# A Perceiver block on one core: self-attention products reordered, five chunks of context values moved

## What is computed

```
x += bitnet_cross_attention(LN(x), ctx)      # ternary weights, int8 activations
x += grouped_rope_attention(LN(x))           # 16 heads of 8, 4 key/value groups, causal   "self-attention 0"
x += mixture_ffn(LN(x))                      # 8 experts merged per token, FF = 512
x += long_attention(LN(x), ctx)              # 16 heads, 32 queries against 512 context tokens
x += causal_attention(LN(x))                 # 16 heads of 8, biases                         "self-attention 1"
x += fourier_linear(LN(x))                   # one 128 x 128 matrix
```

## Time and profile before

| | |
|---|---|
| median of 3 runs | 340.75 us (339.51 to 340.79) |
| the profiled execution, its own time | 340.16 us |
| its span, first to last instruction | 338.3 us |
| mean granted TensorE clock | 0.94 of full |
| PE, DVE, ACT, POOL busy | 80%, 69%, 51%, 15% |
| self-attention 0, from its input on partitions to the sums of its last products | 124.4 to 139.7 us |
| feed-forward layer | 150 to 215 us |
| long attention, from its first query product to its last output | 219 to 299 us |
| self-attention 1 | 306.4 to 323.9 us |

### The profile page before, as it was taken

How to read it: one execution, slowest core, us unless ns; L and a number is a source line. 1 busy time by engine, 2 the same in 40 slices (tenths; PEclk the granted TensorE clock), 3 DMA queues, 4 the chain that set the end, 5 groups by cost and what they waited for, 6 DMA issues and landing times.

```text
span 338.3 us, 7625 instructions
## 1 busy us (share of the span) xinstructions
PE 269.9 (80%) x3085; PEld 163.6 (48%) x3086; DVE 233.5 (69%) x585; ACT 172.0 (51%) x316; POOL 50.7 (15%) x175
## 2 busy tenths in 40 slices
PE   0148686878787999599999999479999999949854
PEld 0113323435343778474445555237567676735742
DVE  4799999986979967349753444577778787275734
ACT  2578896875547554431012000075988888802520
POOL 3115030710000020020002000201322322120002
PEclk9999999899999999779999999987999999976965
DMA  6992000000003999691000000000000000000001
GB/s 169 225 345 100 1 2 0 1 3 2 2 2 77 212 216 241 164 408 43 4 0 0 2 0 0 0 5 0 2 4 4 2 4 4 6 2 0 2 2 31
DMA packets 6315, 19.34 MB, mean 57 GB/s; under 512 B 1157, under 2 KB 2693, under 8 KB 5253
## 3 DMA queue, kind: packets, MB, share of 16 engines
q1 hardware_dynamic: 6277, 18.82, 20.7%
HBM read 12.07 MB, written 0.26 MB: 36 GB/s over the span
## 4 chain that ended last, share of the span: by engine, by line
PE 54%; DVE 27%; ACT 8%; DMA 3%; issue 3%; POOL 3%; SPq 1%; DVEq 0%; ACTq 0%; POOLq 0%
PE PS L1129 50%; DVE sm L763 6%; DMA cx<-ctx_in 3%; DVE sm L700 2%; DVE yq L772 2%; DVE big L821 2%; DVE w L923 2%; DVE sm L922 1%; ACT sa L418 1%; POOL yq L349 1%; DVE yq L830 1%; PE PS L1336 1%; PE PS L1257 1%; ACT yq L418 1%; PE PS L1142 1%
## 5 line engine op out<-in xcount | busy, mean ns | idle before, releaser
L1077 DVE TENSOR_REDUCE sm<-PS 128x1 f32<-128x512 f32 x64 | 42.6, 687 | 14.3 <-PE PS L1129 14.1
L325 POOL TENSOR_TENSOR rstd<-veps,mhalf 128x1 f32<-128x1 f32 x24 | 12.6, 549 | 142.0 <-DVE veps L635 142.0
L1129 PE MATMUL PS<-sa,w 128*32 128x36 f32 (+1 forms) x320 | 30.8, 280 | 2.4 <-ACT w L553 2.4
L600 ACT ACTIVATE yq<-PS,sm 128x512 f32<-128x512 f32 x44 | 29.0, 685 | 5.6 <-PE PS L1129 5.2
L1129 PE MATMUL PS<-yq 128*128 128x384 f32 x96 | 31.1, 486 | 0.0
L530 ACT COPY xT<-PS 128x512 f32<-128x512 f32 x5 | 2.9, 588 | 49.5 <-PE PS L1336 49.5
L418 ACT ACTIVATE big<-PS,cols,sm 128x512 f32<-128x512 f32 (+1 forms) x32 | 26.9, 890 | 1.4 <-PE PS L1129 1.3
L1129 PE MATMUL PS<-big,yq 96*128 96x512 f16 x64 | 24.7, 391 | 2.6 <-ACT yq L418 2.6
L1129 PE MATMUL PS<-yq,big 99*128 99x128 f16 x256 | 24.7, 218 | 1.5 <-ACT yq L604 0.7
L1129 PEld LDWEIGHTS PS<-yq 128*128 128x128 f32 x96 | 18.2, 190 | 12.9 <-issue 0.5
L1129 PEld LDWEIGHTS PS<-yq,big 99*128 99x128 f16 x256 | 18.4, 97 | 11.2 <-issue 3.8
(11 more groups left out here) (253 smaller groups left out, 557.5 us busy)
## 6 DMA issues: line engine op xcount, KB each, us to landing
big<-yq SPq DMA_DIRECT2D x24, 256.0 KB, 5.1
cx<-ctx_in SPq DMA_DIRECT2D x8, 384.0 KB, 13.2
w<-w_in SPq DMA_DIRECT2D x9, 256.0 KB, 4.8
yq<-w_in SPq DMA_DIRECT2D x1, 2304.0 KB, 10.7
wa<-wa_in SPq DMA_DIRECT2D x1, 1156.0 KB, 20.0
sa<-wx_in SPq DMA_DIRECT2D x1, 768.0 KB, 16.1
rows<-rows_in SPq DMA_DIRECT2D x1, 580.0 KB, 17.7
tern<-rows_in SPq DMA_DIRECT2D x1, 512.0 KB, 8.4
```

Of the source, the lines that this page charges most:

```text
L325: pool.tensor_tensor(rstd[:, t:t + 1], veps[:, t:t + 1], mhalf[:, t:t + 1], ALU.pow)\
L600: nc.scalar.activation(pt(i), PS[:, ST_BANK[i % 2], :], ACT.Exp, scale=s1(M_ES))\
L1077: V.tensor_reduce(s1(M_MX + i % 8), PS[:, S_BANK[i % 3], :], AX, ALU.max, negate=True)\
L1129: return nc.tensor.matmul(o, lhsT, rhs, start=start, stop=stop, **kw)
```

## The change

In each self-attention PE lays the masks before it waits for `xT`, makes keys ahead of queries, and makes the values in four quarters (a bank each, in the order 6, 7, 4, 5): one before the scores, one behind them, and the last two between the transposes of the first groups. ACT expands its share of the keys before it reads the queries. It expands the values of banks 6 and 7, two operations after the second exponential and two after the third. Those of banks 4 and 5 are expanded by DVE, behind its two copies of transposed weights, under a new semaphore. The copies of transposed weights of groups 0 and 1 wait for the transposes of groups up to 1 and up to 2; those of groups 2 and 3 for their own, as before.

Of the chunks 11 to 15 of context values, three (`VALUES_AHEAD`) go ahead of the transposes of the third layer norm on PE and, on ACT, ahead of the copy that follows them; two go behind the four products of long queries on PE and behind the last head expansions on ACT. They use banks 5 and 4 in turn, no longer 6 and 5. Nothing is left of them in the loop.

Constants:

```
-                  tuple((c, 5 + c % 2) for c in range(11, NCH)))
+                  tuple((c, 4 + c % 2) for c in range(11, NCH)))
...
-        VALUE_STEPS = [(b, r) for b in range(3) for r in range(1, R)][:len(VALUES[2])]
+        VALUES_AHEAD = 3
```

ACT, the self-attention and the context values:

```
-                act.wait_ge(s["qk_ps"], 2 * k + 1)
-                affine(qTs[:, :], PS[:, 4, :], bias=col(K_Q1) if k else 0.0).then_inc(s["q_ev"], 1)
                 act.wait_ge(s["k_plain"], k + 1)
                 affine(kexp[:, 2, :], mix[:, :], scale=hm[:, 2:3]).then_inc(s["k_eva"], 1)
+                act.wait_ge(s["qk_ps"], 2 * k + 2)
+                affine(qTs[:, :], PS[:, 4, :], bias=col(K_Q1) if k else 0.0).then_inc(s["q_ev"], 1)
...
+                exponential(0)
+                exponential(1)
+                values(0, 2)
+                exponential(2)
+                values(2, 4)
+                exponential(3)
+                for r, transposed in ((1, 3), (3, 4)):
+                    act.wait_ge(s["sa_tp"], R * k + transposed)
                     nc.scalar.copy(wt[:, r, :], PS[:, r, :]).then_inc(s["sa_teva"], 1)
-                    if r == 1:
-                        values(1)
...
             nc.scalar.activation(s1(M_EXP0), s1(M_Z4), ACT.Exp)
+            for step in range(VALUES_AHEAD):
+                context_values(2, step)
             rows_to_features(3)
...
             last_heads(3)
-
+            for step in range(VALUES_AHEAD, len(VALUES[2])):
+                context_values(2, step)
```

DVE, the self-attention:

```
-                dve.wait_ge(s["qk_ps"], 2 * k + 2)
+                dve.wait_ge(s["qk_ps"], 2 * k + 1)
...
-                for r in (0, 2):
-                    dve.wait_ge(s["sa_tp"], R * k + r + 1)
+                for r, transposed in ((0, 2), (2, 3)):
+                    dve.wait_ge(s["sa_tp"], R * k + transposed)
                     V.tensor_copy(wt[:, r, :], PS[:, r, :]).then_inc(s["sa_tevd"], 1)
+                dve.wait_ge(s["v_ps"], 2 * k + 2)
+                src = PS[:, 4:6, :].rearrange("p a (b r c) -> p (a b) r c", b=4, r=R)
+                for h in range(4):
+                    V.tensor_scalar(vexp[:, 0:8, :, 8 * h:8 * h + 8], src[:, :, :, 8 * h:8 * h + 8], rm[:, h:h + 1], None,
+                                    ALU.mult).then_inc(s["v_evd"], 1)
```

PE, the self-attention (the two lines on the masks stand now ahead of the first wait) and the context values:

```
-                pe.wait_ge(s["xt_ev"], (1, 4)[k])
-                mm(PS[:, 4, :], A(q), xT[:, :]).then_inc(s["qk_ps"], 1)
-                mm(PS[:, 5, :], A(kk), xT[:, :]).then_inc(s["qk_ps"], 1)
...
                 for r in range(R):
                     mm(PS[:, r, :], identb[:, :], maskb[:, k, :].unsqueeze(1).broadcast_to([128, 4, 128]), stop=False,
                        skip_group_check=True)
+                pe.wait_ge(s["xt_ev"], (1, 4)[k])
+                mm(PS[:, 5, :], A(kk), xT[:, :]).then_inc(s["qk_ps"], 1)
+                mm(PS[:, 4, :], A(q), xT[:, :]).then_inc(s["qk_ps"], 1)
+
+                def values(n):
+
+                    bank = (6, 7, 4, 5)[n]
+                    for j in range(4):
+                        b = 4 * (bank - 4) + j
+                        last = mm(PS[:, bank, tile(j)], xrep[:, tile(b)], A(v))
+                    if n % 2:
+                        last.then_inc(s["v_ps"], 1)
...
                 values(1)
...
+                transposed(0)
+                values(2)
+                transposed(1)
+                values(3)
+                transposed(2)
+                transposed(3)
...
+            for step in range(VALUES_AHEAD):
+                context_values(2, step)
             rows_to_features(3, xn)
             pe.wait_ge(s["xt_ev"], 3)
             for r in range(R):
                 mm(PS[:, r, :], wa[:, A_WQR + 128 * r:A_WQR + 128 * r + 128], xT[:, :]).then_inc(s["lq_ps"], 1)
+            for step in range(VALUES_AHEAD, len(VALUES[2])):
+                context_values(2, step)
...
-                    if (b, r) in VALUE_STEPS:
-                        context_values(2, VALUE_STEPS.index((b, r)))
```

More of the change, by code:

```diff
@@ L550, in self_attention, with values @@
                         .then_inc(s["sa_exp"], 1)
-                for r in (1, 3):
-                    act.wait_ge(s["sa_tp"], R * k + r + 1)
+                def values(h0, h1):
+                    act.wait_ge(s["v_ps"], 2 * k + 1)
+                    src = PS[:, 6:8, :].rearrange("p a (b r c) -> p (a b) r c", b=4, r=R)
+                    for h in range(h0, h1):
+                        affine(vexp[:, 8:16, :, 8 * h:8 * h + 8], src[:, :, :, 8 * h:8 * h + 8],
+                               scale=rm[:, h:h + 1]).then_inc(s["v_ev"], 1)
+                exponential(0)
[6 more added lines that the diff above has]
+                    act.wait_ge(s["sa_tp"], R * k + transposed)
                     nc.scalar.copy(wt[:, r, :], PS[:, r, :]).then_inc(s["sa_teva"], 1)
-                    if r == 1:
-                        values(1)
                 act.wait_ge(s["ot_ps"], k + 1)
@@ L1340, in self_attention @@
                 q, kk, v, o = ("q1", "k1", "v1", "m1") if k else ("q0", "k0", "v0", "o0")
-                pe.wait_ge(s["xt_ev"], (1, 4)[k])
-                mm(PS[:, 4, :], A(q), xT[:, :]).then_inc(s["qk_ps"], 1)
-                mm(PS[:, 5, :], A(kk), xT[:, :]).then_inc(s["qk_ps"], 1)
-                def values(half):
-                    for b in range(8 * (1 - half), 8 * (2 - half)):
-                        last = mm(PS[:, 4 + b // 4, tile(b % 4)],
-                                  xrep[:, tile(b)], A(v))
-                    last.then_inc(s["v_ps"], 1)
-                pe.wait_ge(s["xrep_ok"], k + 1)
-                values(0)
                 if k == 0:
@@ L1358, in self_attention, with transposed @@
                        skip_group_check=True)
+                pe.wait_ge(s["xt_ev"], (1, 4)[k])
[8 more added lines that the diff above has]
+                        last.then_inc(s["v_ps"], 1)
+                def transposed(r):
+                    pe.wait_ge(s["sa_exp"], R * k + r + 1)
+                    for t in range(T):
+                        last = nc.tensor.transpose(PS[:, r, tile(t)], work[:, r, tile(t)], ident)
+                    last.then_inc(s["sa_tp"], 1)
+                pe.wait_ge(s["xrep_ok"], k + 1)
+                values(0)
                 pe.wait_ge(s["q_ev"], k + 1)
@@ L1369, in self_attention @@
                 values(1)
-                for r in range(R):
-                    pe.wait_ge(s["sa_exp"], R * k + r + 1)
-                    for t in range(T):
-                        last = nc.tensor.transpose(PS[:, r, tile(t)], work[:, r, tile(t)], ident)
-                    last.then_inc(s["sa_tp"], 1)
+                transposed(0)
[4 more added lines that the diff above has]
+                transposed(3)
                 pe.wait_ge(s["vones"], k + 1)
                 for half in range(2):
-                    pe.wait_ge(s["v_ev"], 8 * k + 4 * half + 4)
+                    if half:
+                        pe.wait_ge(s["v_evd"], 4 * k + 4)
+                    else:
+                        pe.wait_ge(s["v_ev"], 4 * k + 4)
                     for r in range(R):
```

14 lines of the change are left out of this document (2 added, 12 removed).

## The result

| | before | changed |
|---|---|---|
| median, 20 runs each | 340.55 us (338.67 to 341.90) | 337.3 us (333.53 to 338.99) |
| ratio | | 0.990, 95% interval 0.9879 to 0.9922 |
| span of the profiled execution | 338.3 us | 335.5 us |
| mean granted TensorE clock in it | 0.940 | 0.927 |

A forecast was written before the change was run, and what follows sets the result against it. The long cross-attention was taken as PE-bound once running, the self-attentions as bound by a chain hopping between engines. Gains 1.0 + 1.4 + 1.8 = 4.2 off 340.16 us gave 336.0, range 333.8 to 338.6.

The forecast's parts named there:

- Self-attention 0: First self-attention: scores start 0.9 sooner and the tail is 0.45 shorter, a gain of 1.35.
- Rival (c): Self-attentions: DVE's four expansions cost 0.75 each, so only the starts gain; 339.0 to 339.5, chance 0.11.
- Between: From self-attention 0 to the feed-forward layer: low clock halves work brought forward, so about 1.0 of 1.35 arrives.
- Self-attention 1: Second self-attention, at the lower clock: start gains 1.4, tail 0.45; gain taken as 1.8.
- the 5 to 6 named: Sign of being right: self-attention 1's scores start 5 to 6 us after the transposed input is copied.
- The long attention: Long cross-attention with chunks 11 to 15 out of its ramp: gain 1.4, bounds 0.3 to 2.6.
- So 2.2 of the 3.3 goes. I take back 0.8: Ramp: wait from split to first transposed scores shrinks from 3.3 to about 1.1; low clock in four transposed steps costs 0.8.
- rival (d): Start of the long cross-attention: low clock persists, 0.5 us per us; slower beyond 8.4 us more of it; chance 0.05.
- the four signs of being wrong: DVE expansions above 0.5; transposes waiting behind value quarters; half-speed transposed scores or outputs; clock low longer in total.
- Rival (b): Queries and ramp: chunks keep PE busy, so no low clock follows; gain 6.1, 334.0, chance 0.12.
- Rival (a): Ramp: scores wait for DVE's maxima and POOL's split, so it gives nothing; gain 3.0, 337.2, chance 0.20.
- The bounds of the terms: Whole kernel: the terms' lower and upper bounds together were said to give gains of 2.0 to 5.9.

The follow-up runs named there:

- sa_only: Changed kernel with the move of the context values undone, so only the self-attentions are changed; 335.9 us, ratio 0.9881.
- hold_outer: Changed kernel with 41 products of constants in PE's waits outside the ramp and none in it; 332.35 us, ratio 0.9737.
- two_in_ramp: Changed kernel with the last two moved chunks back in the ramp, behind the scores of steps 1 and 2; 336.7 us, ratio 0.9882.
- hold_clock: two_in_ramp with 8 products of constants in the ramp and 41 more in PE's other waits; 331.8 us, ratio 0.9750.
- ramp_fill: Changed kernel with 20 products of constants in PE's idle stretches of the ramp; 335.9 us, ratio 0.9883.
- after_again: The changed kernel timed once more as a control, nothing altered; 336.6 us, ratio 0.9904.
- values_only: Kernel before with only the context values moved, both self-attentions as before; 338.7 us, ratio 0.9977.

## Why the prediction was right, and where it was not

*Self-attention 0: right.* 1.35 was forecast, 1.48 measured (0.95 + 0.53). Each step holds: keys at 124.87, scores at 128.10 and released by DVE's key expansions, quarters hidden, and the last products released by DVE's value expansions. Their size, taken from the row of two 128x256 operations in the earlier trace rows, was 0.37 and is 0.41; ACT's, put at 0.37 as well where the earlier trace rows have 1.57 for four, are 0.41 too. Rival (c), at 0.75 each, is out. The Trainium skill's rule in "VectorE: DVE Perf Modes", section "Mode 2×_2P", that only a source in SBUF gives the doubled rate, agrees: from PSUM 256 elements take 0.41, where 512 from SBUF take 0.43.

*Between: right in this pair of executions.* Of 1.48, 1.18 reached the feed-forward layer (10.29 became 10.59); 1.0 was forecast of 1.35. The reason given, that work brought forward into a stretch at the lower clock runs at half speed there, is borne out by the kernels with the clock held, where this way takes 8.71 without the change and 8.73 with it, so that nothing is lost. How close 0.30 came to the 0.35 forecast is partly luck: the way took 9.3 to 10.8 in the other profiled executions without products of constants around it, by the length of the low stretch in it.

*Self-attention 1: right, and low by some 0.4.* Forecast 1.4 + 0.45, measured 1.72 + 0.48; scores start 5.1 after the input is copied, within the 5 to 6 named. The size of the start depends on the clock: transposes to scores took 7.3 to 7.8 in the kernels with the change at the lower clock. With the clock at full it is 5.90. The kernel before was not caught there with its clock up for the whole start, so what the change is worth there at full clock is not shown; the 0.95 of self-attention 0, which has the same steps, is an estimate for it.

*The long attention: wrong.* The step that failed is in the paragraph on chunks 11 to 15: "So 2.2 of the 3.3 goes. I take back 0.8". Measured, in the profiled executions, is a loss of 0.65 where a gain of 1.4 stood (0.1 to 0.65 over all of them). It has two parts. The order is worth 1.25 (77.87 with the chunks in the ramp, 76.62 with them out of it, both at full clock from the first scores on), not 2.2. The end of that step was right: without chunks, and at full clock, 1.10 lies between split and transposed scores, and 1.1 was forecast (1.39 in the changed kernel). Its start was not: of the 3.3 read off the profile, 1.0 was the lower clock under those very chunks. And the low stretch cost 2.7 (79.29 against 76.62), not 0.8: the prediction had it over with the first four transposed steps, and it went on through the start of the full pipeline, until 242. That end was named as the lower bound of the term (0.3) and, beyond it, in rival (d). Rival (d) had the right place and the wrong price: the low stretches at this place grew from 3.4 to 13.7 us, by 10.3, past the 8.4 from which (d) said that the change would lose, but each us cost about 0.2 (1.90 over 10.3, where 1.90 is 2.67 less the 0.77 by which before and sa_only differ) and not 0.5. In most of the ramp PE waits for DVE and ACT at either clock, and the 10.4 us of low clock ahead of the first outputs cost 1.4. The last 3.2, in the full pipeline, cost 1.26, that is 0.4 each, near (d)'s price.

Two of the four signs of being wrong that the prediction named were seen: transposed scores and outputs at half speed beyond the first b, and a clock that is low for longer in total (mean 0.927 against 0.940). Rival (b), that the clock holds, was seen in none of the profiled executions with the chunks moved and no products in the ramp. Rival (a), that the ramp gives nothing, has the number nearest to the median, 337.2, but not the mechanism: at full clock the order is worth 1.25 and not (a)'s 0.2, and it was the clock that took it back.

Taken together, by stages of the profiled executions the forecast was -4.2 and the measurement -2.9. The difference of 1.3 is +2.05 in the long attention and +0.30 behind it, against -0.18 in self-attention 0 and the way behind it, -0.40 in self-attention 1 and -0.46 in the tail. The 0.30 and the 0.46 are in the same program as before, where the clock changed at other moments; no step of the prediction was about them, and that they nearly cancel is luck. The bounds of the terms, added up as they stand in the prediction, give gains of about 1.9 to 6.3, not 2.0 to 5.9.

The Trainium skill's rule in "TensorE: Matmul & The Clock Gate", section "Why this matters for your kernels", that long idle gaps cost the clock, would have given the three chunks ahead of the layer norm a gain of 1 us. The trace disagrees on that place: with the gap filled up to 215.1 and a transpose at 215.42, the clock fell at 218.05 (0.52 in 218:220). The price was right where the clock did hold: in hold_outer, which has the same program there, the four products of queries took 3.70, not 5.40, and the first transposed scores came 16.65 behind the transposes, not 17.86. That the same program kept the clock once and lost it in the other profiled executions shows that the gap alone does not decide it. In the ramp it fell at about 228.3 without one long gap: no wait of PE between 225.15 and 228.93 was above 1.28 (three rows above: 1.28, 0.59, 0.94). So a rule on single gaps did not tell either fall here.

Open is how the 3.3 us of the medians divide. The stages divide the 2.8 of one execution; single executions of the changed kernel spread over 5.5 us, those of the kernel before over 3.2.

## What to carry to other kernels

Before moving dense products off an engine that "has too much to do" in a ramp, ask what clock it will have once they are gone: here the order was worth 1.25 us and the lower clock took 2.7. Durations read off a stretch at the lower clock are not the price of the work; find the same rows at full clock first. And where PE waits often and briefly between dependent small steps, products of constants in its waits were worth more than the whole reordering (3.3): 41 of them brought 4.7 us on the kernel before and 4.2 to 5.0 on the changed one; 56, with two of the chunks back in the ramp, 6 to 7. And one profiled execution cannot price a change while the clock moves between executions: here single executions of one kernel spread over 3.2 and 5.5 us.

## What was not expected of the hardware

*The clock stayed low, and fell, while PE was busy.* In the changed kernel PE is busy for 2.00 of 2.00 us in each window from 232 to 242 and its clock stays at 0.50. The work in it is scores (96 rows, f16), transposed scores and rows of maxima, and the clock came back only after output products had begun. In the kernel before, at the same place, it came back at 232.5, behind two fp32 chunks. But the kind of work does not tell either: in two_in_ramp it came back at 234.9, with scores, transposed scores and rows of maxima alone since 231.1, and 2.1 ahead of the first output products. And hold_clock lost its clock in the middle of a self-attention that it had entered at full, right behind the scores of 32x32 tiles; windows of its profiled execution, with the timeline of PE:

```profile
304.00:306.00 2.00, 1.62 (x10) 1.05 (x8) 1.96 (x5) 1.28 (x2) 0.00 (x0) 1.00 0.00 0
306.00:308.00 2.00, 1.91 (x100) 1.93 (x108) 0.74 (x2) 0.01 (x1) 0.00 (x0) 1.00 0.00 0
308.00:310.00 2.00, 2.00 (x52) 1.80 (x35) 1.97 (x4) 0.63 (x1) 0.00 (x0) 0.73 0.03 8
```

```profile
306.10 2.76 PE L1139 MATMUL PS<-sa,qTs 32*32 32x128 f32 x128 [0.47 <-ACT qTs L419]
308.78 1.99 PE L1139 MATMUL PS<-wa,w 128*128 128x128 f32 x8
```

PE was busy 1.91 of 2.00 before the fall; the quarter of values behind it took 1.99 instead of 1.16, and the self-attention, from its scores to its last value products, 11.69 instead of 10.11. In hold_outer, with the same self-attention, the clock did not fall there. So PE's busy time in the profile did not tell at these places what the clock would do. What does was not tested and is open.

*The first scores of the ramp start late.* In the changed kernel they come 1.28 after the last chunk, at 226.43, although ACT's head expansion for them had ended at 223.69. In ramp_fill, where five products of constants follow the chunks and end at 226.81, they come 1.13 later still, and ACT had been done since 224.27. With no products put there (two_in_ramp) PE waits 0.18 behind its last work, and for ACT. The timelines of PE in ramp_fill and in two_in_ramp:

```profile
223.78 1.95 PE L1139 MATMUL PS<-wa,cx 97*128 97x128 f32 x16
225.57 1.24 PE L1139 MATMUL PS<-noff 128*128 128x512 bf16 x5
227.95 0.59 PE L1139 MATMUL PS<-big,yq 96*128 96x512 f16 x2 [1.13 <-ACT yq L419]
```

```profile
218.03 4.77 PE L1138 MATMUL PS<-xT,wa 128*128 128x512 f32 x7
222.98 0.38 PE L1138 MATMUL PS<-big,yq 96*128 96x512 f16 x1 [0.18 <-ACT yq L418]
```

In the other profiled executions with two chunks there the same wait was 0.63 (after_again), 1.01 (values_only) and 1.11 (hold_outer), each time with ACT long done. The loop of these scores stands behind a branch on a value in memory, and a delay of 0.6 to 1.3 behind products that are placed right ahead of a branch would fit; no run took the branch away, so the cause is open. The result does not hang on it: DVE's first maximum comes 12.56 behind the transposes, and 12.44 before. The 8 products of the later kernels all stand inside the loop.
